# Edge attributes stored as 64 rows in place of 51, and loaded into 64 partitions

## What is computed

```python
# layer 0
agg = segment_sum(edge_weight[:, None] * x[src], dst)
x   = layernorm(x + relu((x + agg) @ W1 + b1) @ W2 + b2)
# layer 1, edges
h1 = x @ lin1_w.T
c  = 0.5 * (cos(edge_weight * pi / 10) + 1)
z1 = edge_attr @ nn_w1.T + nn_b1                  # edge_attr: 412500 x 50
s  = softplus(z1) - log 2
W  = (softplus(s @ nn_w2.T + nn_b2) - log 2) * c[:, None]
h2 = h1 + segment_sum(W * h1[dst], src)
# layer 1, nodes
x  = layernorm(x + h2 @ lin2_w.T + lin2_b)
```

## Time and profile before

| | |
|---|---|
| time, median of 3 runs | 11676.23 us (11665.03 to 11705.83) |
| span of the profiled execution | 11664.8 us, 0.2 us under the fastest of the three runs |
| PE, DVE, POOL, ACT busy, share of the span | 59%, 56%, 54%, 29% |
| attribute loads (L373) | 403 of 204.0 KB |
| stores of hid (L365), zero blocks (L378), each tile | 512.0 KB and 264.0 KB |
| DMA over the span | 131 GB/s |

### The profile page before, as it was taken

One profiled execution on the slowest core, in us unless ns is written; L12 is line 12 of the kernel. 1 busy time (PEld: TensorE's weight loads), 2 busy tenths in 40 slices (PEclk: granted clock), 3 DMA queues, 4 the chain that ended last, 5 costly groups with the idle time before them and its releaser, 6 DMA issues. The chain is left out here.

```text
span 11664.8 us, 216512 instructions
## 1 busy us (share of the span) xinstructions
PE 6895.8 (59%) x38816; PEld 4956.1 (42%) x38817; DVE 6516.8 (56%) x20428; ACT 3390.7 (29%) x6781; POOL 6346.0 (54%) x6541
## 2 busy tenths in 40 slices
PE   2555566565555666665444456666666666666666
PEld 1333333333333333334232345555555555555566
DVE  7666666666666655555333345555555555555555
ACT  2333333333333333334222222222222222222202
POOL 3666566665666566652555555555555565555500
PEclk8777776777777777778776678888888888888887
DMA  3333343433333333443333344444444444444444
GB/s 101 124 121 123 119 124 122 124 121 120 122 124 121 120 124 123 124 122 123 99 100 98 100 133 150 149 149 156 150 152 146 151 156 148 157 151 151 153 155 151
DMA packets 803242, 1533.31 MB, mean 131 GB/s; under 512 B 193070, under 2 KB 206820, under 8 KB 802707
## 3 DMA queue, kind: packets, MB, share of 16 engines
q1 hardware_dynamic: 593415, 1093.58, 28.8%
q0 software_dynamic: 209456, 436.16, 13.0%
q10 hardware_dynamic: 348, 3.33, 0.1%
HBM read 967.92 MB, written 564.58 MB: 131 GB/s over the span
## 5 line engine op out<-in xcount | busy, mean ns | idle before, releaser
L1232 POOL DMA_INDIRECT sorted_messages<-rows,sidx x3224 | 3261.3, 1012 | 2621.7 <-DVE sidx L1279 1433.0
L434 POOL DMA_INDIRECT xg<-x_rows,gidx x3224 | 3043.0, 944 | 2134.8 <-PE bank L477 1112.7
L483 PE MATMUL bank<-attr,nn 128*128 128x512 f32 x1612 | 1494.2, 1082 | 1764.1 <-DMA attr<-attr_cols 1501.9
L1158 PE MATMUL bank<-hot,block_rows 128*128 128x128 f32 x9312 | 1586.3, 341 | 248.6 <-DVE hot L1314 140.7
L1185 ACT ACTIVATE soft<-bank 128x512 f32<-128x512 f32 x806 | 481.4, 597 | 4079.1 <-remote 2654.4
L1158 PEld LDWEIGHTS bank<-hot,block_rows 128*128 128x128 f32 x9312 | 1507.6, 254 | 299.4 <-issue 285.2
L1128 PE MATMUL bank<-w_nn2T,e_hid 128*128 128x128 f32 x6448 | 1057.4, 309 | 610.4 <-DMA e_hid<-hidden 349.0
L483 PEld LDWEIGHTS bank<-attr,nn 128*128 128x128 f32 x1612 | 468.9, 321 | 2225.7 <-issue 2061.2
L1285 DVE SCALAR_TENSOR_TENSOR rows<-filt,meta,bank 128x128 f32<-128x128 f32 x3224 | 916.6, 344 | 809.7 <-remote 534.8
L1128 PEld LDWEIGHTS bank<-w_nn2T,e_hid 128*128 128x128 f32 x6448 | 977.4, 219 | 816.7 <-DMA e_hid<-hidden 481.1
L397 ACT ACTIVATE soft<-bank 128x512 f32<-128x512 f32 x808 | 475.4, 588 | 2751.7 <-issue 1841.9
(11 more groups left out here) (182 smaller groups left out, 8173.3 us busy)
## 6 DMA issues: line engine op xcount, KB each, us to landing
block_rows<-sorted_messages SPq DMA_DIRECT2D x389, 792.0 KB
hidden<-hid SPq DMA_DIRECT2D x404, 512.0 KB
e_hid<-hidden SPq DMA_DIRECT2D x403, 512.0 KB
sorted_messages<-zero SPq DMA_DIRECT2D x403, 264.0 KB
dstb<-dst SPq DMA_DIRECT2D x403, 256.0 KB
attr<-attr_cols SPq DMA_DIRECT2D x403, 204.0 KB
xg<-x_rows,gidx POOLq DMA_INDIRECT x3224
sorted_messages<-rows,sidx POOLq DMA_INDIRECT x3224
```

The costliest lines, as they stand in the source:

```text
L434: pool.indirect_dma_start(xg[s][:, :], None, x_rows, bass.IndirectOffsetOnAxis(ap=gidx[s // HALF][:, s % HALF:s % HALF + 1], axis=0),).the ...
L483: nc.tensor.matmul(bank[2 + h][:, :], nn1[:, :], attr[:, h, :], start=True, stop=True).then_inc(z1_set, 1)
L1158: ins = nc.tensor.matmul(sums[u][:, 0:P], block_rows[k][:, u, s, 0:D], hot[u][:, s, :], start=(s == 0), stop=(s == HALF - 1))
L1232: pool.indirect_dma_start(table, bass.IndirectOffsetOnAxis(ap=sidx[b][h][:, s:s + 1], axis=0), rows[b][h][:, s, :], None).then_inc(landed[ ...
```

## The change

The host makes 64 rows in place of 51; rows 51 to 63 are zeros. The load takes all 64 rows into 64 partitions. Nothing else is changed: the same matmuls read the same 128 partitions, the same semaphores are waited for.

```diff
+ATTR_ROWS = 64
...
-                                sp.dma_start(attr[0:GAUSS + 1, :, :].rearrange("a h e -> a (h e)"), attr_cols[:, ds(t * TE, TE)]).then_inc(attr_in, 16)
+                                sp.dma_start(attr[0:ATTR_ROWS, :, :].rearrange("a h e -> a (h e)"), attr_cols[:, ds(t * TE, TE)]).then_inc(attr_in, 16)
...
-    at = np.zeros((1 + GAUSS, EPAD), attr.dtype)
+    at = np.zeros((ATTR_ROWS, EPAD), attr.dtype)
     at[0] = 1
-    at[1:, :E] = attr.T
+    at[1:1 + GAUSS, :E] = attr.T
```

## The result

The changed kernel takes 11738.43 us (median of 20 runs, 11704.73 to 11761.87), the kernel before 11705.62 us beside it (20 runs, 11661.27 to 11731.07): ratio 1.003, 95% interval 1.002 to 1.004. It is slower by 0.3%, some 33 us. The forecast was 11660.

The account below looks back on a forecast made before the run. The prediction took POOL's gathers and their release, 12.4 us a tile, to bound layer 0's edge stage. Gains of 7 us (late tiles) and 9 us (part ends) gave -16 us and a median of 11660 us; range 11,560 to 11,700.

Parts of the forecast that it names:

- What bounds the kernel: Layer 0's edge stage: POOL's gathers and their release set the 12.4 us tile; PE's 1501.9 us attribute wait is off the path.
- POOL's ring: Layer 0's edge stage: eight gathers of 8.74 us plus 3.65 us until the next tile's first gather, 12.39 us a tile.
- rival B: Edge stage: PE sets the tile after all, so the earlier attribute matmul saves 685 us, about 10,990; chance 0.03.
- Spread and landing: Attribute load: 16 engines in place of 3, landing 2.8 us after issue instead of 5.29, L483 2.5 us into the tile.
- rival C: Attribute load: 64 partitions still use 3 engines, landing takes 6.64 us, 302 us slower, about 11,980; chance 0.05.
- The sign named for it: Attribute matmul L483: its wait on the DMA was to fall from 1501.9 us to under 150 us.
- Late tiles: Edge stage: 35 tiles whose L483 starts 5.0 to 5.4 us in become normal, 0.2 us each, 7 us saved.
- Ends of parts: Three part ends, where planning stands behind L483 and no gather covers it: 3 us saved at each, 9 us.
- The sum of the gains: Whole kernel: 7 us from tiles with a late L483 and 9 us from part ends, -16 us in all.
- Gathers and other DMAs: SP's DMAs in the edge stage: same three at the same places, new load gone before the first gather's rows; given nothing.
- Normal tiles: 0: Ordinary edge-stage tiles: an earlier L483 gains nothing, as the attribute wait has slack; bound 9 us.
- Rival A: Tile ends: taking the load off three overloaded engines shortens each tile by 0.24 us, 97 us, about 11,560; chance 0.15.

Follow-up runs that it names:

- 52 rows with the late zero block: Changed kernel with 52 rows and one more satisfied SP wait before it sends the zeros; 0.9996 and, in a later set, 0.9981 of the kernel before.
- held-back run: Changed kernel, 64 rows, with both halves of the attribute matmul L484 waiting for the second half of hid; ratio 1.0013 to the kernel before.

## Why the prediction was wrong, by its steps

- *What bounds the kernel.* Right. POOL's ring sets the tile, and PE's wait for the attributes is off it: 379 us of that wait went and the stage got no shorter by it. With three rows the stage shrank by 17.8 us, not by rival B's 685.
- *Spread and landing.* Right in kind. 3 engines became 16, rival C is refuted, and the last packet took 2.69 us against the 2.8 taken for the landing. But L484 starts 2.88 us into the tile, not 2.5: it begins 0.94 us after the last packet is down (0.60 before the change), and the first row came 0.4 us later than with 51 rows. The sign named for it, a wait on the DMA of under 150 us, was no good sign. 1269.2 us were left, but 1041.7 are left with 52 rows too, whose L484 starts at 2.54 us, the same place as with three rows, where the same idle time has no DMA as its end:

```profile
L484 PE MATMUL bank<-attr,nn 128*128 128x512 f32 x1612 | 1504.1, 1088 | 1246.1 <-DMA attr<-attr_cols 1041.7
L483 PE MATMUL bank<-attr,nn 128*128 128x512 f32 x1612 | 1501.0, 1086 | 1242.0 <-issue 1210.8
```

- *Late tiles.* Right: some 35 tiles had L483 past 5.0 us before, and none after. But with 57 rows, where the load is slower, only 6 are left, so a quicker load isn't the only thing that removes them.
- *Ends of parts.* Right in sign, under half in size: with 52 rows the three part-end tiles went from 18.70, 19.38 and 19.68 to 17.94, 17.96 and 17.89 us, 4.0 us together where 9 stood. With the forecast's 64 rows it is 2.2 us, with 57 rows 1.9, and the second profile of the kernel before is 0.9 below the first.
- *The sum of the gains.* -16 us was forecast. The stage shrank by 13.9 us with 52 rows, by 10.0 and 14.5 with 65 (the second against the second profile of before), by 17.8 with three, but also by 7.4 with 57 rows. That the sum was met so closely with 52 and 65 rows is in part luck.
- *The step that failed* is "Gathers and other DMAs. SP issues the same three DMAs at the same places [...] I give that nothing", and with it "Normal tiles: 0". SP did not issue them at the same places: the new load's record is 0.19 us longer, its packets begin 0.39 us later after the issue, and in the median tile of the first three quarters it goes out 0.2 us nearer to the tile's first gather. Its reason, that the new load has left the engines before the first gather's rows fly, didn't hold either: in the median tile the last row is down 1.95 us into the tile and the first gather's first row starts at 1.74. The term measured +0.16 us a tile in the median, 0.11 in the mean with the late tiles' gain in it: the fourth part starts 35.0 us later (3985.7 against 3950.7), 1.9 of it from before the stage, and the last quarter and its start give 3.6 back, +31.4 in all. Which of these differences costs the time isn't shown; 52 rows with the late zero block are issued as late without a loss, the held-back run has the long record without most of it, and its rows still fly when the first gather's begin (1.78 against 1.65 us).
- *Rival A* looked at the same place with the other sign. It took it that the end of a tile reacts to where SP's load stands and was given a chance of 0.15; that a tile could get longer there had no case, and that is why slower had only 0.09. Its evidence was weaker than it looked: the earlier trace rows is the end of one of the 14 us tiles (2991.02 to 3005.14), in which the gathers stand at other times than in a normal tile.

Shown: among loads of 3, 48, 51, 52, 57, 64 and 65 rows the loss comes with 64 alone (three profiles, from three sets of runs). Bytes, the number of engines, the earliness of L484, the lateness of the zero block and the lateness of the load itself are each excluded as the only cause by a run that has them without the loss. Seen within runs, not by an edit: with 64 rows a tile is longer where its load was issued later. Not shown: why 64 rows take SP longer to issue than 65 or 80, whether the late issue or the early L484 is needed beside them, and by what path such a load holds back a release that comes more than ten microseconds later. The last quarter, where SP's load goes out about a microsecond ahead, is spared; that fits the issue time and proves nothing. Sizes such as 60, 63, 96 or 128 rows weren't run.

65 rows do what 64 were to do: 0.9976 [0.9962, 0.9989] in one set, 0.999 [0.9975, 1.0005] in the other. The stage gains 10 to 15 us, which is 0.1% of the whole; I would take it as a small gain, at the edge of what can be measured.

## What to carry to other kernels

When a wait off the path gets shorter, don't put the rest of the change at nothing: here a transfer nearly twice as fast cost 0.3%, and one row more or 12 fewer didn't. After a change of a DMA's shape, look also at the duration of its issue record, at when it is issued and at its first packet, and not only at when its data land; here they were the first signs that 64 rows are different, though not the proven cause. Try the neighbouring sizes before explaining a loss by a general mechanism: 52 and 65 rows told within one set each that neither the spread nor the bytes cost anything. And test a sign on a run in which you know the answer: with 52 rows the profile put over 1000 us of waiting down to a DMA whose last packet was down 1.1 us before the wait ended.

## What the runs showed of the hardware

- The issue record of this load takes 324 ns for 51 rows, 323 for 57, 322 for 3, 353 for 48 of 64, 389 for 52, 391 for 65, 355 for 80, and 515 for 64; the first packet comes 0.90 to 0.98 us after the issue for all the others and 1.30 for 64 (medians, the record over the stage).
- The number of packets that end the DMA was 3 for 51, 57 and 3 rows, 13 for 52 and 65, 16 for 48, 64 and 80: the rule of the Trainium skill, page "DMA: Bandwidth & Descriptors", section "Why a DMA increments its semaphore by 16 and not by 1", says that a DMA issued by SP runs on the largest number of engines up to 16 that divides the slowest dimension of both sides, here the rows, and that each of these engines ends with a write to the semaphore. These eight sizes agree.
- Two of the five further sets ran where the kernel before takes 11798 and 11815 us in place of 11699 to 11711, with tiles of 12.56 to 12.61 in all six profiles taken there. The kernel before has no profile there. The last quarter's stretch of the earlier trace rows there, with 52 rows and the late zero block:

```profile
L436 POOL DMA_INDIRECT xg<-x_rows,gidx x401: 938/944/994, 4330.1 to 4959.4; - x134
```

  It holds 401 gathers, where the same kernel had 408 on the other chip. A comparison of stage lengths across such sets would read this as a cost of the edit; a profile of the kernel before from the same set guards against it.
